# A loop over the sequences, written out on four engines: a conditioning and feed-forward kernel of 32 sequences

## What is computed

```python
# conditioning, 16 heads of 16 channels
query = seq2 + b_self
key = concatenate([seq1 + b_prev, seq2 + b_self], 1)
value = concatenate([seq1, seq2], 1)
# scores against the first 256 keys (masked by length), one more score of each token with itself
attn = softmax(score) @ v, then attn @ Wo + bo
# two layers, 8 heads of 64 channels, window 128
h = shift_token(x); q, k, v = split(h @ wqkv); q, k normalised and rotated
x = x + local_attention(q, k, v) @ wo
h = layernorm(shift_token(x)); a, g = split(h @ w1 + b1)
x = x + (a * gelu(g)) @ w2 + b2
```

## Time and profile before

| what | us |
| --- | --- |
| median of 3 runs (4104.72 to 4107.03) | 4105.37 |
| the profiled execution, its own time | 4102.22 |
| its span, first to last instruction | 4100.1 |
| DVE busy | 2793.1 (68%) |
| ACT busy | 2343.0 (57%) |
| POOL busy | 786.1 (19%) |

### The profile page before, as it was taken

One profiled execution on the slowest core, in us unless ns is written; L12 is line 12 of the kernel. 1 busy time (PEld: TensorE's weight loads), 2 busy tenths in 40 slices (PEclk: granted clock), 3 DMA queues, 4 the chain that ended last, 5 costly groups with the idle time before them and its releaser, 6 DMA issues.

```text
span 4100.1 us, 70276 instructions
## 1 busy us (share of the span) xinstructions
PE 3832.6 (93%) x22372; PEld 2562.4 (62%) x22372; DVE 2793.1 (68%) x7663; ACT 2343.0 (57%) x5248; POOL 786.1 (19%) x976
## 2 busy tenths in 40 slices
PE   6799999999999999999999999999999999999987
PEld 3456666666666666666666666666666666666655
DVE  3577677667677767677767767767767767767653
ACT  2355556655656655656655656655656655656552
POOL 1122122112122112122112122212122212122100
PEclk6799999999999999999999999999999999999997
DMA  3000000000000000000000000000000000000000
GB/s 116 6 11 7 5 11 11 11 11 6 6 11 11 11 11 6 6 11 11 11 11 6 6 11 11 11 11 6 6 11 11 11 11 6 6 11 6 6 6 8
DMA packets 48277, 46.55 MB, mean 11 GB/s; under 512 B 8716, under 2 KB 46816, under 8 KB 48096
## 3 DMA queue, kind: packets, MB, share of 16 engines
q1 hardware_dynamic: 48096, 44.87, 3.5%
HBM read 35.69 MB, written 8.39 MB: 11 GB/s over the span
## 4 chain that ended last, share of the span: by engine, by line
PE 40%; issue 38%; DVE 11%; POOL 7%; ACT 2%; DVEq 0%; POOLq 0%; DMA 0%; SPq 0%; ACTq 0%
PE ps L981 6%; POOL inv L549 5%; PE ps L876 5%; PE ps L890 4%; PE ps L734 4%; PE ps L952 3%; PE ps L932 2%; PE ps L943 2%; PE ps L791 2%; PE ps L816 2%; PE ps L923 2%; PE ps L910 1%; DVE feed_area L1260 1%; DVE attn_area L1190 1%; DVE ssq L1194 1%
## 5 line engine op out<-in xcount | busy, mean ns | idle before, releaser
L981 PE MATMUL ps<-feed_area,w_s 128*128 128x256 f32 x2560 | 595.2, 384 | 7.4 <-DVE feed_area L1262 6.3
L549 POOL TENSOR_TENSOR inv<-ssq_f,minus_half 128x16 f32<-128x16 f32 x128 | 419.2, 3275 | 946.3 <-DVE ssq_f L1198 946.3
L647 ACT ACTIVATE attn_area<-attn_area,f_nb,inv 128x128 f32<-128x128 f32 (+1 forms) x1024 | 546.1, 538 | 22.7 <-DVE f_nb L1226 21.9
L981 PEld LDWEIGHTS ps<-feed_area,w_s 128*128 128x128 f32 x2560 | 479.2, 192 | 92.9 <-issue 16.8
L1135 DVE TENSOR_REDUCE c_mx<-ps 128x2 f32<-128x512 f32 x512 | 343.6, 688 | 142.2 <-PE ps L763 138.9
L600 ACT ACTIVATE cond_area<-ps 128x512 f32<-128x512 f32 x512 | 299.2, 598 | 240.3 <-PE ps L781 232.8
L1222 DVE CUSTOM_DVE_ANT_0 attn_area<-ps,cst 128x128 f32<-128x128 f32 (+1 forms) x1024 | 304.1, 353 | 148.3 <-issue 148.3
L1272 DVE SCALAR_TENSOR_TENSOR feed_area<-ps,b_s,feed_area 128x256 f32<-128x256 f32 (+1 forms) x384 | 184.5, 481 | 268.1 <-ACT feed_area L669 262.1
L994 PE MATMUL ps<-feed_area,w_s 128*128 128x256 f32 x1536 | 355.3, 381 | 0.7 <-DVE feed_area L1272 0.7
L638 ACT ACTIVATE attn_area<-ps 128x512 f32<-128x512 f32 x256 | 152.9, 597 | 323.3 <-PE ps L910 320.5
L669 ACT ACTIVATE feed_area<-ps,b_s 128x256 f32<-128x256 f32 x320 | 150.9, 472 | 311.6 <-PE ps L981 311.2
(11 more groups left out here) (150 smaller groups left out, 7113.1 us busy)
## 6 DMA issues: line engine op xcount, KB each, us to landing
x_rows<-in_x SPq DMA_DIRECT2D x32, 256.0 KB, 2.7
f_rows<-in_fside_BxSxS SPq DMA_DIRECT2D x32, 256.0 KB, 3.0
res_rows<-in_x SPq DMA_DIRECT2D x32, 256.0 KB, 2.8
out<-res_rows SPq DMA_DIRECT2D x32, 256.0 KB, 2.6
wqkv_s<-in_L_ffn_wqkv SPq DMA_DIRECT2D x2, 1536.0 KB
w_s<-in_L_ffn_w SPq DMA_DIRECT2D x2, 1364.0 KB
cond_area<-cond_area SPq DMA_DIRECT2D x128, 6.0 KB
w_s<-in_L_ffn_w SPq DMA_DIRECT2D x2, 640.0 KB
```

Source lines behind the costliest of these rows:

```text
L549: nc.gpsimd.tensor_tensor(inv[:, l, t, :], ssq_f[:, l, t, :], minus_half[:, :], ALU.pow).then_inc(SL[l]["inv_norm"], 1)
L647: nc.scalar.activation(soft[:, h % SOFT, lo:hi], soft[:, h % SOFT, lo:hi], ACT.Exp, bias=f_nb[:, l, q, h:h + 1], scale=inv[:, l, q, h:h + ...
L981: last = mm(ps[:, N0 + f % 2, c * N:(c + 1) * N], w1_s[:, l, k, lo:lo + P], hn[:, k, :], start=(k == 0), stop=(k == KD - 1))
```

## The change

The loop is gone on the four engines of `run`: `static(i)` is called for all 35 passes, so each round of the loop becomes a stretch of program of its own, with constants in its waits. The steps, their order and their instructions on each engine stay as they were. SyncE's program is not touched.

```diff
@@ -383,12 +383,7 @@
                             layers_setup()
                             layers[0] = True
 
-            for i in range(LAGS):
-                static(i)
-            with eng.Fori(0, seqs - LAGS) as first:
-                for lag, name, n in body:
-                    step(first + (LAGS - lag) if lag < LAGS else first, name, n)
-            for i in range(seqs, seqs + LAGS):
+            for i in range(seqs + LAGS):
                 static(i)
 
         def copy_probs(eng, copy, seq, l, h):
```

## The result

Writing the passes out on all four engines takes the median from 4105.05 us to 3975.91 us (four runs each), a ratio of 0.969 with a 95% interval of 0.9672 to 0.9707. The forecast was 3980 us. The profiled execution took 3978.39 us, where the sum had given 3976.9.

The account below looks back on a forecast made before the run. PE, busy 93%, bounds the kernel, so only its idle or slow time can be won: 84.0 us of stalls plus 41.3 of slow clock, 125.3 off 4102.22, gives 3976.9; plus 3.2 to the median, 3980 us, range 3960 to 4002.

Parts of the forecast that it names:

- DVE's stall at the jump: DVE idles after its loop branch and PE waits before L890: 3.00 us for each of 28 jumps, 84.0 us.
- the fall-through: End of the last round, where DVE's branch doesn't jump: PE waits only 0.17 us before L890, 2.50 us from L952's group.
- Nothing else differs between the two places: Claim that L890 after a jump (5.50 us from L952's group) and after the last round (2.50) differ only by the jump.
- The slow clock behind it: Half clock granted for a short while after most of PE's idle stretches at the jump: 41.3 us, some 1.5 a jump.
- Rival A: The slow clock stays or comes back elsewhere, as at PE's 1.19 us pause before L932: 4021 us, half 4001; chance 0.07.
- Register commands: Loop commands on DVE, PE, ACT and POOL (92, 85, 74, 27 a round) claimed hidden behind PE's own pace: 0 us.
- rival B: Register commands were in the way, so PE's 1.19 and 0.80 us waits shrink: 3922 us, a third 3961; chance 0.07.
- the four small waits: PE's waits of 7.1, 5.9, 4.9 and 4.5 us in 28 rounds, 0.80 us a round; gain bounded by 22.4 us, taken as 0.
- A wait that the change adds: Claimed none: where two waits stood on a register command and an instruction, they would stand on the instruction.
- PE's fetches: PE's written-out program fetches 6 packets of 16 KB a pass, claimed to arrive in time: 0 us.
- rival C: PE starves on late 16 KB fetches, 168 crossings: 4551 us, small form 3997; chance 0.02 slower than no change, 0.04 small.
- the reading of queue 8 and queue 14: Instruction queues in the loop: queue 8, read as PE's, moves nothing; queue 14 moves 133 packets, near 5 a round.

Follow-up runs that it names:

- the mirror: PE, ACT and POOL written out while DVE keeps its loop, against the looped kernel: 4108.81 us, ratio 1.0013.
- 13 jumps in place of 28: All four loops kept, but DVE's round holds two passes, against the looped kernel: 4033.18 us, ratio 0.9834.
- the delays without a jump: The full change plus a useless DVE reduction ahead of L1245 in 29 passes: 128x3072 gave 4114.14 us, 128x1024 gave 4003.77 us.
- the hint: All four loops kept, with a prefetch instruction for DVE's jump at the head of each round, against the looped kernel: 3974.57 us, ratio 0.9689.
- the moved edge: All four loops kept, DVE's loop boundary moved to behind layer 1's first feed-forward step in the same order of work: 3968.0 us, ratio 0.9673.

## Why the prediction was right

**DVE's stall at the jump, 84.0 us.** Right. DVE alone written out gives the gain, the mirror gives none, and 13 jumps in place of 28 give half. The changed kernel has the 2.50 us from L952's group to L890 on which the 3.00 us a jump rested. The step that held was to take the fall-through as the state after, and not the whole wait of 3.17 us. "Nothing else differs between the two places" was not so, though: see the wait below.

**The slow clock behind it, 41.3 us.** Right, and the delays without a jump show it by themselves: 3.4 us of pause bring it back, 1.26 don't. Rival A, that it would come up elsewhere, didn't happen: the granted clock is 1.00 over the middle passes.

**Register commands, 0.** Right. The 33.4 us before L927 stayed, so rival B is out. With DVE's loop and every register command kept, a pass takes 117.97 us with the hint, with the moved edge and with the head at 0, just what it takes with DVE alone written out. Of the four small waits one got shorter in the changed kernel (before L714, 0.21 to 0.14 us) and one longer (before L938, 7.1 to 8.2 us in all); in the length of a pass these shifts don't show.

**A wait that the change adds, "None".** Wrong, by 0.1 us a pass. With all passes written out a pass takes 118.07 us, against the 117.97 with PE's loop kept. The trace shows where. The two waits of this step in the changed kernel, then with DVE alone written out (PEldq is PE's sequencer; 29 of the rows are the loop's):

```profile
L883 PEldq EVENT_SEMAPHORE  x63: 51/51/51, 244.6 to 3900.4; - x63
...
L892 PEldq EVENT_SEMAPHORE  x34: 51/51/51, 244.9 to 3897.4; - x34
L892 PEldq FUSED_REGOPS  x29: 37/37/37, 287.6 to 3591.2; - x29
```

and PE's timeline with DVE alone written out:

```profile
2174.08 1.89 PE L956 MATMUL ps<-attn_area,wo_s 128*128 128x256 f32 x8
...
2176.49 1.98 PE L894 MATMUL ps<-wqkv_s,X_ffn 128*128 128x512 f32 x4
```

In the loop the first of the two waits stands on a register command that PE has done long before, and the weight load of L894 waits for DVE itself. Written out, the wait for DVE gets an instruction of its own ahead of the weight load. From the end of DVE's addition to the matmul it is then 0.15 us instead of 0.05, and from L947's group 2.50 us instead of 2176.49 - 2174.08 = 2.41. So about half of the 0.17 us that the prediction gave to "the work between" is this instruction. It did no harm to the number, because the fall-through stands in front of a written-out pass and holds the same instruction. The jump itself costs 121.06 - 117.97 = 3.09 us, and the written-out PE gives 0.09 of that back: 29 x 0.1 = 3 us, as the mirror's ratio of 1.0013 says too.

**PE's fetches, 0.** Right as far as the runs show. The full change fetches 184 packets, rival C's stall isn't there, and the 0.10 us a pass are explained by the wait instruction.

**The sum.** The profiled execution came out at 3978.39 us against 3976.9, 1.5 us above; the 29 passes account for 0.7 of it, the filling for 0.9. The median lies 4 us below the 3980. Two of four runs took 3973.3 and two 3978.4, so the 3.15 us that I added for the distance from execution to median weren't there.

**One of the signs failed in one pass.** PE's wait before L885 was to be at most 0.2 us in every pass; it is 0.17 in all but one and 0.43 in that.

**What else was wrong without changing the number** is the reading of queue 8 and queue 14: "its body stays in the engine, and DVE's doesn't". That sounds like a body too long for the engine. A body of 353 instructions stays as well, if it is laid at the start of a block. The prediction didn't need the cause of the late instruction, only that straight code hasn't got it, which the fall-through had shown.

## What to carry to other kernels

Look at every engine's branch in the profile and at the first instruction behind it: here 0.3 us was a healthy jump and 3.5 us a fetch, and PE, waiting behind that engine, paid it in each round. Before writing a loop out, try the cheap cures, a hint on the jump or the loop's head at the start of a fetch block: here they gave 3974.57 and 3974.83 us with the loop kept, against 3975.91. And since a change of a few instructions ahead of a loop may move its body from a good place to a bad one, a jump of 3% after a harmless edit is worth this look.

## What the runs showed of the hardware

- The same loop body of 353 instructions on DVE jumps in 0.3 us with its head laid at slot 0 of a fetch block and in 3.4 us with its head at slot 64. The times are 3974.83 and 4101.98 us.
- The packets that fetch DVE's program carry 8 KB, and in the round with the head at 64 they follow the borders of pieces of 128 instructions. Without a hint, bodies that touch three pieces stayed and bodies that touch four were fetched again, five packets a round.
- The hint didn't bring a fetch forward, it stopped the repeated fetches: none from 424 to 3590 us, where the loop without it had 127.
- The clock granted to PE fell to half behind most pauses of 3.2 to 3.4 us and behind none of 1.2 to 1.3 us, at the very same place of the pass. With 13 jumps, 9 had a slow stretch behind them; with 28, 25 had; with 29 delays and no jump, 28 had.
- Where the matmul at L885 waits for two semaphores, the trace has a wait instruction of its own (51 ns) ahead of the weight load. It made PE start 0.09 us later behind DVE's addition.
